# Layer 0 of a two-layer graph network: one power for norm and inverse deviation, the gate's tanh in its PSUM bank, and the mix reads the projection in PSUM

## What is computed

```
norm  = (sum(adj, -1) + 1e-6) ** -0.5
f_hom = adj @ ((x @ theta) * norm) * norm
f_het = x @ W_h
gate  = sigmoid(x @ W_t + b_t)
out   = elu(gate * f_hom + (1 - gate) * f_het)
x     = layernorm(x + out)
```

## Time and profile before

| | us |
|---|---|
| median of 3 runs | 2246.25 (2244.37 to 2246.46) |
| the profiled execution | 2246.6 |
| its span, first to last instruction | 2244.8 |
| mean granted TensorE clock, share of full | 0.974 |
| busy: PE, DVE, ACT, POOL | 2039.8, 1470.5, 1175.7, 676.7 |

### The profile page before, as it was taken

One profiled execution on the slowest core, in us unless ns is written; L12 is line 12 of the kernel. 1 busy time (PEld: TensorE's weight loads), 2 busy tenths in 40 slices (PEclk: granted clock), 3 DMA queues, 4 the chain that ended last, 5 costly groups with the idle time before them and its releaser, 6 DMA issues.

```text
span 2244.8 us, 38042 instructions
## 1 busy us (share of the span) xinstructions
PE 2039.8 (91%) x11782; PEld 1745.0 (78%) x11782; DVE 1470.5 (66%) x2709; ACT 1175.7 (52%) x2174; POOL 676.7 (30%) x563
## 2 busy tenths in 40 slices
PE   6888788885988789884999999999999999999997
PEld 5877687774888677774888888888888888888886
DVE  5999797996777666654555655565656565555564
ACT  6888687874555566553344444444444444434342
POOL 5887686873000000000222222222222222222222
PEclk9999999997999999996999999999999999999999
DMA  4655565564222387774112112121212121212110
GB/s 143 220 203 203 191 211 212 213 220 168 80 80 84 88 238 231 230 211 160 45 58 75 66 66 74 58 77 54 78 53 78 53 78 53 78 53 80 67 38 19
DMA packets 208069, 263.07 MB, mean 117 GB/s; under 512 B 12939, under 2 KB 159089, under 8 KB 203761
## 3 DMA queue, kind: packets, MB, share of 16 engines
q1 hardware_dynamic: 207984, 262.14, 35.2%
HBM read 174.01 MB, written 88.08 MB: 117 GB/s over the span
## 4 chain that ended last, share of the span: by engine, by line
PE 52%; issue 1%; ACT 1%; DMA 1%; DVE 0%; SPq 0%; POOL 0%; POOLq 0%; ACTq 0%; DVEq 0%
PE c_ps_g L1386 36%; PE c_ps_s L1413 5%; PE c_ps_m L1386 4%; PE c_ps_s L1386 2%; PE c_ps_s L1457 1%; PE c_ps_y L1436 1%; PE c_ps_y L1473 1%; PE c_ps_m L1473 1%; DMA c_yf<-y_spec 1%; PE c_ps_m L1474 0%; PE c_ps_y L1474 0%; ACT c_wi_h L1147 0%; SPq L1038 0%; SPq L1046 0%; DVE c_t L1255 0%
## 5 line engine op out<-in xcount | busy, mean ns | idle before, releaser
L1209 POOL TENSOR_TENSOR c_cl<-c_xc,c_ch 128x512 fp32r<-128x512 f32 x64 | 82.6, 1291 | 488.2 <-ACT c_ch L1101 470.8
L1285 DVE TENSOR_SCALAR c_work<-c_work 128x512 f32<-128x512 f32 x64 | 27.4, 427 | 219.3 <-ACT c_work L1096 219.3
L833 PE MATMUL m_ps<-m_wh,m_xl 128*128 128x256 f32 (+1 forms) x406 | 136.4, 336 | 35.1 <-issue 16.8
L1386 PE MATMUL c_ps_g<-c_xh,c_wh_l 128*128 128x512 f32 x384 | 155.6, 405 | 4.2 <-POOL c_cl L1209 4.2
L1386 PE MATMUL c_ps_g<-c_ch,c_wi_l 128*128 128x512 f32 x384 | 153.9, 401 | 0.0
L1386 PE MATMUL c_ps_g<-c_xl,c_wh_h 128*128 128x512 f32 x384 | 152.4, 397 | 0.0
L1386 PE MATMUL c_ps_g<-c_ch,c_wi_h 128*128 128x512 f32 x384 | 152.1, 396 | 0.0
L1386 PE MATMUL c_ps_g<-c_nh,c_wi_l 128*128 128x512 f32 x384 | 151.9, 396 | 0.0
L1386 PE MATMUL c_ps_g<-c_xh,c_wh_h 128*128 128x512 f32 x384 | 151.9, 396 | 0.0
L1386 PE MATMUL c_ps_g<-c_cl,c_wi_h 128*128 128x512 f32 x384 | 151.7, 395 | 0.0
L1386 PE MATMUL c_ps_g<-c_nl,c_wi_h 128*128 128x512 f32 x384 | 151.7, 395 | 0.0
(11 more groups left out here) (226 smaller groups left out, 7095.9 us busy)
## 6 DMA issues: line engine op xcount, KB each, us to landing
w_spec<-a_spec SPq DMA_DIRECT2D x32, 1088.0 KB, 11.0
m_w<-w_spec SPq DMA_DIRECT2D x68, 512.0 KB, 3.8
a_xt<-in_x_t SPq DMA_DIRECT2D x64, 256.0 KB
a_xn<-in_x_n SPq DMA_DIRECT2D x64, 256.0 KB, 9.3
x_t<-a_x1t SPq DMA_DIRECT2D x64, 256.0 KB, 9.7
s_x<-x_t SPq DMA_DIRECT2D x64, 256.0 KB, 3.0
y_spec<-m_y SPq DMA_DIRECT2D x64, 256.0 KB, 2.4
c_x<-x_t SPq DMA_DIRECT2D x32, 512.0 KB, 3.9
```

The lines of the kernel that those rows point to most:

```text
L833: last = nc.tensor.matmul(out.rearrange("p r (q c) -> p r q c", q=CHUNKS), xx[:, v, c, part], ww[:, v, c].rearrange("p q r c -> p r q c")[ ...
L1209: nc.gpsimd.tensor_tensor(cl[:, v, j], xc[:, j], ch[:, v, j].bitcast(F32), ALU.subtract).then_inc(s_cl, 1)
L1285: nc.vector.tensor_scalar(zz[:, :], tz[:, :], 0.5, 0.5, ALU.mult, ALU.add).then_inc(s_zz, 1)
L1386: last = nc.tensor.matmul(out, stationary, moving, start=(n == 0), stop=(n == len(passes) - 1))
```

## The change

The powers of `norm` (pair i - 2) and `rstd` (now of pair i - 6, at the start of the next step instead of the end of this one) become one instruction over four columns: the sums under the roots stand side by side in `sums_eps`, the results in `roots`. The tanh of the gate is written back to `ps_g`, where VectorE's `gd` reads it; the tile `gate` is gone. `mix` reads f_het from `ps_hh` and no longer from the copy `het`, which stays for `diff`. So the banks are freed later: `ps_g` by `gd`, `ps_hh` by `mix`. The rest follows from the names.

```diff
@@ tiles
-        deg_eps = sb("deg_eps", [P, 2])
-        norm = sb("norm", [P, 2, 2])
+        sums_eps = sb("sums_eps", [P, 4])
+        roots = sb("roots", [P, 2, 4])
+        deg_eps, var_eps = sums_eps[:, 0:2], sums_eps[:, 2:4]
...
-        gate = sb("gate", [P, 2, 2, D])
...
-        neg_half = sb("neg_half", [P, 2])
-        var_eps = sb("var_eps", [P, 2])
-        rstd = sb("rstd", [P, 2, 2])
+        neg_half = sb("neg_half", [P, 4])
@@ ScalarE
-                    nc.scalar.activation(fh[:, u, b], ps_hh[:, 2 * u + b, 0:D], ACT.Copy, scale=norm[:, u, b:b + 1]).then_inc(s_fh, 1)
+                    nc.scalar.activation(fh[:, u, b], ps_hh[:, 2 * u + b, 0:D], ACT.Copy, scale=roots[:, u, b:b + 1]).then_inc(s_fh, 1)
...
-                    reached(act, s_rstd, p)
-                    nc.scalar.activation(var_eps[:, :], mv[:, v, :, 1], ACT.Identity, bias=eps[:, 0:1]).then_inc(s_ve, 1)
+                    reached(act, s_root, p + 4)
+                    nc.scalar.activation(var_eps, mv[:, v, :, 1], ACT.Identity, bias=eps[:, 0:1]).then_inc(s_ve, 1)
...
                     reached(act, s_gp, p2 + 1)
-                    reached(act, s_gd, p2 - 1)
-                    nc.scalar.activation(gate[:, u], ps_g[:, :, :], ACT.Tanh, scale=0.5).then_inc(s_gate, 1)
+                    nc.scalar.activation(ps_g[:, :, :], ps_g[:, :, :], ACT.Tanh, scale=0.5).then_inc(s_gate, 1)
@@ GpSimd
-                if live(2):
-                    p = i - 2
-                    reached(pool, s_dege, p + 1)
-                    reached(pool, s_diff, p - 1)
-                    reached(pool, s_fl, p - 1)
-                    nc.gpsimd.tensor_tensor(norm[:, u], deg_eps[:, :], neg_half[:, :], ALU.pow).then_inc(s_norm, 1)
+                if live(2) or live(6):
+
+                    if live(2):
+                        reached(pool, s_dege, i - 1)
+                        reached(pool, s_diff, i - 3)
+                        reached(pool, s_fl, i - 3)
+                    if live(6):
+                        reached(pool, s_ve, i - 5)
+                        reached(pool, s_x1, i - 7)
+                    these = slice(0 if live(2) else 2, 4 if live(6) else 2)
+                    nc.gpsimd.tensor_tensor(roots[:, u, these], sums_eps[:, these], neg_half[:, these], ALU.pow).then_inc(s_root, 1)
...
-                if live(5):
-                    p = i - 5
-                    reached(pool, s_ve, p + 1)
-                    reached(pool, s_x1, p - 1)
-                    nc.gpsimd.tensor_tensor(rstd[:, v], var_eps[:, :], neg_half[:, :], ALU.pow).then_inc(s_rstd, 1)
@@ VectorE
-                    nc.vector.scalar_tensor_tensor(gd[:, :, :], gate[:, v], 1.0, diff[:, :, :], ALU.add, ALU.mult).then_inc(s_gd, 1)
+                    nc.vector.scalar_tensor_tensor(gd[:, :, :], ps_g[:, :, :], 1.0, diff[:, :, :], ALU.add, ALU.mult).then_inc(s_gd, 1)
...
-                    nc.vector.scalar_tensor_tensor(mix[:, v], gd[:, :, :], 0.5, het[:, v],
+                    nc.vector.scalar_tensor_tensor(mix[:, v], gd[:, :, :], 0.5, ps_hh[:, 2 * v:2 * v + 2, D:2 * D],
                                                    ALU.mult, ALU.add).then_inc(s_mix, 1)
                 if live(6):
-                    reached(dve, s_rstd, p6 + 1)
+                    reached(dve, s_root, p6 + 5)
@@ TensorE
                         reached(pe, s_fl, p2 - 1)
-                        reached(pe, s_het, p2 - 1)
+                        reached(pe, s_mix, p2 - 1)
...
                 if live(2):
-                    reached(pe, s_gate, p2)
+                    reached(pe, s_gd, p2)
                     nc.tensor.matmul(ps_g.rearrange("p b d -> p (b d)"), ones[:, :], bt_rows.rearrange("p b d -> p (b d)"), start=True, stop=False)
```

More of the change, by code:

```diff
@@ L138, in phase_a @@
         s_dege = sem("degree_eps")
-        s_norm = sem("norm")
+        s_root = sem("norm_and_rstd")
         s_proj = sem("projected")
@@ L157, in phase_a @@
         s_ve = sem("var_eps_done")
-        s_rstd = sem("rstd_done")
         s_x1 = sem("x1_done")
@@ L236, in f_high @@
                         reached(act, s_hom, p2 - 1)
-                        reached(act, s_norm, p2 + 1)
+                        reached(act, s_root, p2 + 1)
                     reached(act, s_proj, 2 * p2 + b + 1)
-                    nc.scalar.activation(fh[:, u, b], ps_hh[:, 2 * u + b, 0:D], ACT.Copy, scale=norm[:, u, b:b + 1]).then_inc(s_fh, 1)
+                    nc.scalar.activation(fh[:, u, b], ps_hh[:, 2 * u + b, 0:D], ACT.Copy, scale=roots[:, u, b:b + 1]).then_inc(s_fh, 1)
                 def spectra_out(c):
@@ L358, in step @@
                     reached(dve, s_deg, p2 + 1)
-                    reached(dve, s_norm, p2)
-                    nc.vector.tensor_scalar(deg_eps[:, :], ps_deg[:, :, 0], 1e-6, None, ALU.add).then_inc(s_dege, 1)
+                    reached(dve, s_root, p2)
+                    nc.vector.tensor_scalar(deg_eps, ps_deg[:, :, 0], 1e-6, None, ALU.add).then_inc(s_dege, 1)
                 if live(5):
@@ L369, in step @@
                     for b in range(2):
-                        last = nc.vector.scalar_tensor_tensor(diff[:, b], ps_hom[:, b], norm[:, v, b:b + 1], het[:, v, b],
+                        last = nc.vector.scalar_tensor_tensor(diff[:, b], ps_hom[:, b], roots[:, v, b:b + 1], het[:, v, b],
                                                               ALU.mult, ALU.subtract)
@@ L392, in step @@
                     reached(dve, s_gd, p3 + 1)
-                    nc.vector.scalar_tensor_tensor(mix[:, v], gd[:, :, :], 0.5, het[:, v],
+                    nc.vector.scalar_tensor_tensor(mix[:, v], gd[:, :, :], 0.5, ps_hh[:, 2 * v:2 * v + 2, D:2 * D],
                                                    ALU.mult, ALU.add).then_inc(s_mix, 1)
                 if live(6):
-                    reached(dve, s_rstd, p6 + 1)
+                    reached(dve, s_root, p6 + 5)
                     reached(dve, s_tr, p6 - 1)
                     for b in range(2):
-                        last = nc.vector.tensor_scalar(x1[:, u, b], y[:, u, b], mv[:, u, b, 0:1], rstd[:, u, b:b + 1],
+                        last = nc.vector.tensor_scalar(x1[:, u, b], y[:, u, b], mv[:, u, b, 0:1], roots[:, u, 2 + b:3 + b],
                                                        ALU.subtract, ALU.mult)
@@ L412, in step @@
                     for b in range(2):
-                        last = nc.vector.scalar_tensor_tensor(fl[:, u, b], ps_hh[:, 2 * u + b, 0:D], norm[:, u, b:b + 1],
+                        last = nc.vector.scalar_tensor_tensor(fl[:, u, b], ps_hh[:, 2 * u + b, 0:D], roots[:, u, b:b + 1],
                                                               fh[:, u, b].bitcast(F32), ALU.mult, ALU.subtract)
```

## The result

The changed kernel takes 2250.22 us in the median (2248.46 to 2252.88, 13 executions), the kernel before 2245.39 beside it (2243.9 to 2247.54, 13). The ratio is 1.0022, with a 95% interval of 1.0014 to 1.0031: slower by 4.8 us, small but clear of zero. The profiled execution has a span of 2250.1 us at a granted clock of 0.971, 5.3 us more than the one before.

The account below looks back on a forecast made before the run. It took the DMAs' pace, 8.05 us a step, to bound layer 0 until about 500 us; only -1.7 us behind that took 2246.6 to 2244.9, and the median's 0.35 made 2244.5 us, range 2236 to 2249.

Parts of the forecast that it names:

- the sum: Total of the terms: compute gains 0.46 us a step, but only the time behind 499.50 us shortens, by 1.7 us.
- the x1t at 499.50: ScalarE's x1t instruction that waits for a store late in layer 0; claimed to stay at 499.50 us.
- One power for two: GpSimd's two powers a step merged over four columns: worth 0, at most 0.1 us a step or +6 us.
- PSUM reads: VectorE's gd and mix with one PSUM input: 0.72 us each, al 1.19 to 0.75, res 1.74 to 1.26.
- The circle: Compute's dependency loop over two steps through ScalarE, GpSimd, VectorE and TensorE, without slack: 7.54 to 7.08 us a step.
- the rival in which compute sets the pace everywhere: Some 60 steps gain 0.46 us each: -27 us, 2219 us; chance 0.13.
- The two paces: Over 16 steps of layer 0 from 128 us, DMA and compute (130.6 us) claimed equal within 2 us.
- The waits of x1t: ScalarE's waits for x1t stores between 128 and 260 us: claimed to grow to at least three times 8.1 us.
- TensorE's new waits: Gate matmul waits for gd with 1.05 us to spare, projection for mix with 3 us: both claimed 0.
- The one rival on the slow side: TensorE's gate matmul waits for gd if one PSUM read takes over 1.8 us: 2252 us; chance 0.05.
- The signs given for a wrong forecast: The 16 a_xn loads from 128 us on taking under 127 us, or L481 showing waits for gd.
- the 3 us named: Claim that layer 0 ends within 3 us of where it does now.

Follow-up runs that it names:

- experiment 3: 64-byte idle tile ahead of the taps' buffer: changed kernel 2245.4 us (second tile behind that buffer: 2244.97), kernel before 2252.5, kernel before with merged power alone 2246.75.
- experiment 5: One taps load a step, buffer 128 bytes behind a multiple of 256: changed kernel 2209.81 us, PSUM reads with two powers 2208.01; last, on a multiple of 512, 2208.16.
- experiment 2: Each half of the change alone on the kernel before: merged power 2252.63 us; tanh in place with gd and mix reading PSUM, two powers kept, 2243.73 us.
- experiment 1: Three taps loads a step of 34 partitions replaced by one of 102: kernel before 2224.36 us, changed kernel 2213.43 us.

## Why the prediction was wrong

*The step that failed* stands in the sum: DMA "moves the same bytes in the same order", "so the x1t at 499.50 stays where it is". It came at 503.49:

```profile
503.49 0.60 ACT L281 ACTIVATE a_x1t<-a_ps_t 128x512 f32<-128x512 f32 x1 [2.34 <-DMA x_t<-a_x1t]
```

Bytes and order were the same, but the destination was not: the tiles that the merged power replaces moved the taps' buffer from 128 to 64 bytes behind a multiple of 256, and the DMA chain, which the prediction rightly took as the pace, ran 5 us later by pair 59. The term "One power for two", "Worth 0", priced the instruction and its wait, and not the tiles. So the forecast of 2244.5 us, with 2249 as the upper end, met 2250.22. The swaps of experiment 3 show it in both directions: 5 us off the changed kernel, 6 to 7 us onto the kernel before. With `gr` held 128 behind, the change gives -0.4 us with an interval of -2.5 to +1.6 (0.9998, 0.9989 to 1.0007), and the sum's -1.7 lies in it.

*What the merged power costs by itself* was nearly right. With the buffers in like places it is 0.3 us on the kernel before (2246.75 against 2246.42), and 1.7 and 1.8 us with the PSUM reads (2245.4 against 2243.73, 2209.81 against 2208.01); none of these is clear of zero. The length was off: 1.37 to 1.42 us, not 1.02 to 1.1. The timeline above has y, with two SBUF inputs, beside it, and in the last profile of experiment 5 norm in the same place takes 1.07 where rstd takes 0.71. The difference, 0.36, is about that between 1.37 and 1.02, 0.35. But in the kernel before rstd took 1.03. That y is what stretches the merged power is read from this, not tried.

*PSUM reads:* gd 0.674 and mix 0.689 for 0.72, al 0.77 and res 1.34 to 1.38 for 0.75 and 1.26. By the Trainium skill's page "VectorE: DVE Perf Modes", section on the TRN2 errata, each would have been dearer by some 65 ns, an estimate from its fixed cycles; gd from PSUM takes 0.674 and from SBUF, alone, 0.67, so this kernel does not show it. The term of the sum, -1.7 us, measured -2.7 with an interval of -0.7 to -4.7 (experiment 2).

*The circle:* 7.54 to 7.08 us was too much; it came to 7.3. Without the change it held, 7.5 us a step with the one taps load too. With the change the wait for fl is gone from TensorE, and its own work with the wait for ScalarE's spectra copy takes over at 7.3 (experiment 1). So the rival in which compute sets the pace everywhere, -27 us, could not have come out at more than the 11 to 15 us that experiments 1 and 5 give without the DMA bound.

*The two paces* were not "equal within 2 us". The prediction had compute at 130.6 us for 16 steps, 10 of them lost at a loop end. In experiment 1, where SyncE waits for compute in every step, the inputs of pairs 12 and 28 land at 114.3 and 235.6 us on the kernel before: 121.3 us for 16 steps, and 123.5 for the next 16. A loop end costs compute some 3 us and not 10; the rest belonged to the DMAs' pace. That compute's gain would vanish was therefore better founded than the prediction knew, and the one taps load brought 22 us and not 8 to 15.

*The waits of x1t* did not grow threefold from 128 to 260 us, but from 8.1 to 11.2 us. Threefold did not follow from the prediction's own numbers: 16 steps at 0.46 us are 7.4 us, which makes 15.5. And a part went to another place: GpSimd's res waits 7.0 us for its input xn in that stretch, where it waited 1.8.

*TensorE's new waits:* none for gd, as predicted. The one rival on the slow side had its chance for a mechanism that did not occur; the cause that did was on no list. The signs given for a wrong forecast did not fire either, since the 16 loads from pair 12 to 28 took 131.1 us. Layer 0 ended 3.2 us later, by the last res, just outside the 3 us named.

## What to carry to other kernels

Where DMAs set the pace, a change of tiles is a change of addresses: list where each DMA's buffer starts before and after, and hold them equal with an idle tile before judging anything else. Try the SBUF buffers that a busy DMA engine writes on multiples of 256 bytes: here it is shown for one of them, written by loads over 34 partitions, while the buffers of `xt`, `at` and `xn` stand 160 bytes behind one in all runs and were not moved. And spread a load over many DMA engines first, which was worth 22 us here and left little of the cost of a badly placed buffer; compute gains show only behind that.

## What was not expected of the hardware

- The start of an SBUF buffer of 8192 bytes a partition, on a multiple of 256 or 64 to 192 bytes behind one, moves a DMA-bound kernel by 10 to 16 us, up to 0.7% (2236.15 and 2252.5 us on the kernel before).
- The places off the multiple are not equal: 128 behind costs 10 us, 96 behind 12, 64 behind 15 (changed kernel), and 192 behind 6 to 7 more than 128 (kernel before).
- One GpSimd power over four columns takes 1.37 us in this step and 1.02 in layer 1; over two columns 1.03 to 1.07 or 0.71; what beside it decides this was not tried.
